# Running maximum of attention scores read from the SBUF copy instead of the PSUM bank

## The reference, cut to what matters

```python
kv = jnp.concatenate([context, latents], axis=1)        # 1857 rows of 512
q, k, v = latents @ Wq, kv @ Wk, kv @ Wv                # split into heads
q, k = rms_norm(q, q_norm_w), rms_norm(k, k_norm_w)
scores = jnp.einsum('bhgqd,bhkd->bhgqk', qg, k) / np.sqrt(128)
probs = jax.nn.softmax(scores, axis=-1)                 # max over the keys first
out = jnp.einsum('bhgqk,bhkd->bhgqd', probs, v)         # then out @ Wo
```

## Time and profile before

| what | value |
|---|---|
| median of three runs | 2953.23 us |
| the profiled execution's own time | 2952.19 us |
| its span, first to last instruction | 2950.4 us |
| busy: PE, DVE, ACT, POOL | 2800.4, 2178.1, 2069.0, 2418.5 us |
| mean granted TensorE clock | 0.965 of full speed |

### The profile page before, as it was taken

One profiled execution on the slowest core, in us unless ns is written; L12 is line 12 of the kernel. 1 busy time (PEld: TensorE's weight loads), 2 busy tenths in 40 slices (PEclk: granted clock), 3 DMA queues, 4 the chain that ended last, 5 costly groups with the idle time before them and its releaser, 6 DMA issues. The chain is left out here.

```text
span 2950.4 us, 46837 instructions
## 1 busy us (share of the span) xinstructions
PE 2800.4 (95%) x14860; PEld 2242.9 (76%) x14860; DVE 2178.1 (74%) x3447; ACT 2069.0 (70%) x3867; POOL 2418.5 (82%) x2271
## 2 busy tenths in 40 slices
PE   4669999999999999999999999999999999999976
PEld 2458888888888888888888888888888888888744
DVE  5677777777777777777777778777777777777855
ACT  2137777777777777777777777777777777777741
POOL 4548888888888888888988888888898888888880
PEclk7779999999999999999999999999999999999985
DMA  6224434333434433333434343334334333333101
GB/s 236 90 93 143 144 128 139 127 127 129 147 122 157 133 130 131 132 131 130 143 125 154 129 137 132 129 127 138 127 122 138 113 115 113 109 108 115 65 8 68
DMA packets 154885, 367.69 MB, mean 125 GB/s; under 512 B 12682, under 2 KB 46476, under 8 KB 154641
## 3 DMA queue, kind: packets, MB, share of 16 engines
q1 hardware_dynamic: 152888, 362.87, 37.1%
q10 hardware_dynamic: 1752, 1.84, 0.2%
HBM read 327.95 MB, written 36.70 MB: 124 GB/s over the span
## 5 line engine op out<-in xcount | busy, mean ns | idle before, releaser
L1170 DVE SCALAR_TENSOR_TENSOR running_max<-S_ps,rk,running_max 128x512 f32<-128x512 f32 (+1 forms) x896 | 669.6, 747 | 251.0 <-ACT scores L912 243.2
L912 ACT ACTIVATE scores<-S_ps,rk 128x512 f32<-128x512 f32 (+1 forms) x960 | 653.8, 681 | 225.9 <-PE S_ps L652 220.9
L570 POOL TENSOR_TENSOR P_lo<-late,P_hi 128x512 fp32r<-128x512 f32 x512 | 675.2, 1319 | 129.2 <-ACT late L928 129.2
L1154 DVE TENSOR_TENSOR scores<-scores,Mb_ps 128x512 f32<-128x512 f32 (+1 forms) x960 | 648.8, 677 | 166.4 <-PE Mb_ps L797 166.4
L588 POOL TENSOR_TENSOR late<-late,scores 128x512 f32<-128x512 f32 (+1 forms) x448 | 587.4, 1311 | 119.5 <-ACT scores L928 76.9
L650 PE MATMUL S_ps<-QT_hi,KT_hi 128*128 128x512 f32 (+1 forms) x960 | 560.3, 584 | 15.1 <-DVE running_max L1170 13.9
L588 POOL TENSOR_TENSOR late<-late 128x512 f32<-128x512 f32 x384 | 525.0, 1367 | 0.0
L650 PE MATMUL K_ps<-Wkv_hi,kvT 128*128 128x256 f32 (+1 forms) x1664 | 473.6, 285 | 2.9 <-DVE V_full L1210 2.9
L652 PE MATMUL K_ps<-Wkv_hi,kvT 128*128 128x256 f32 (+1 forms) x1664 | 473.7, 285 | 0.0
L651 PE MATMUL K_ps<-Wkv_lo,kvT 128*128 128x256 f32 (+1 forms) x1664 | 473.1, 284 | 0.0
L680 PE MATMUL OT_ps<-scores,V_full 128*128 128x512 f32 (+1 forms) x896 | 462.1, 598 | 0.0
(11 more groups left out here) (198 smaller groups left out, 5447.7 us busy)
## 6 DMA issues: line engine op xcount, KB each, us to landing
kvT<-kvT_scratch SPq DMA_DIRECT2D x416, 512.0 KB, 3.3
w_stage<-in_L_xattn_Wq SPq DMA_DIRECT2D x64, 512.0 KB, 4.3
w_stage<-in_L_xattn_Wo SPq DMA_DIRECT2D x64, 512.0 KB, 4.3
kvT_scratch<-built SPq DMA_DIRECT2D x58, 512.0 KB, 2.8
xrow<-in_ctx SPq DMA_DIRECT2D x48, 256.0 KB
w_stage<-in_L_xattn_Wk SPq DMA_DIRECT2D x32, 256.0 KB, 2.8
w_stage<-in_L_xattn_Wv SPq DMA_DIRECT2D x32, 256.0 KB, 3.3
xT<-kvT_scratch SPq DMA_DIRECT2D x6, 512.0 KB, 5.7
```

The costliest lines, as they stand in the source:

```text
L570: e.tensor_tensor(P_lo[n % 2][0:r, :], P_sb[n % 2][0:r, :], f(P_hi[n % 2][0:r, :]), ALU.subtract)\
L912: e.activation(row[s % RING][0:r, :], S_ps[s % 2][0:r, :], ACT.Copy, scale=rk[0:r, v % 2, j:j + 1])\
L1154: e.tensor_tensor(d, d, Mb_ps[0:r, :], ALU.add).then_inc(s_d, 1)
L1170: e.scalar_tensor_tensor(a, src, k, a, ALU.mult, ALU.max).then_inc(s_top, 1)
```

## The change

`raise_max` takes its source from the ring slot that ACT's copy has just filled instead of from the PSUM bank. The slot holds the scaled scores, so the multiplication by `rk` goes: the `scalar_tensor_tensor` of 14 tiles of a half becomes a `tensor_tensor` maximum of two SBUF operands, and the `tensor_scalar` of the first tile becomes a `tensor_copy` from SBUF to SBUF. DVE's running maximum no longer reads the bank, so PE's wait before it fills a bank again is on `s_cp` (ACT's copy of two steps before) instead of `s_top`. `rk` is no longer read by DVE, so POOL's wait on `s_top` before it writes `rk` goes too. Every engine has the same number of instructions in the same places as before.

```diff
@@ newton (POOL)
                 if kind != "q" and v >= 2:
 
                     e.wait_ge(s_cp, NJ * (2 * v - 2))
-                    e.wait_ge(s_top, NJ * (2 * v - 2))
                 e.tensor_tensor(r, a, y0, ALU.mult).then_inc(s_nw, 1)
@@ scores (PE)
                 if s >= 2:
 
-                    e.wait_ge(s_top, s - 1)
+                    e.wait_ge(s_cp, s - 1)
@@ raise_max (DVE)
                 a = top[0:r, :]
                 e.wait_ge(s_cp, s + 1)
-                src, k = S_ps[s % 2][0:r, :], rk[0:r, v % 2, j:j + 1]
+                src = row[s % RING][0:r, :]
                 if j == 0:
                     if p:
 
                         e.wait_ge(s_ff, F_AT["MT", p - 1] + 1)
-                    e.tensor_scalar(a, src, k, None, ALU.mult).then_inc(s_top, 1)
+                    e.tensor_copy(a, src).then_inc(s_top, 1)
                     return
                 e.wait_ge(s_top, s)
-                e.scalar_tensor_tensor(a, src, k, a, ALU.mult, ALU.max).then_inc(s_top, 1)
+                e.tensor_tensor(a, a, src, ALU.max).then_inc(s_top, 1)
```

## The result

The changed kernel takes 3142.24 us (median of four runs, 3140.86 to 3146.86) against 2952.64 us before (median of the three runs above and one beside it): 1.0645 times as long, 95% interval 1.063 to 1.0659. The forecast was 3175 us, slower, in a range of 3035 to 3345.

What follows compares the result with a forecast made beforehand. PE bounds the kernel at 83.7 us a unit; POOL would become the bound at 73.4 + 3.0 + 12.1 + 2.4 = 90.9, +7.2 over 31 units: 2952.2 + 223 = 3175 us, range 3035 to 3345.

Steps and rivals of the forecast that it cites:

- The maximum takes turns with POOL: DVE's maximum with two SBUF inputs and POOL's SBUF instructions run one after the other; maximum 1.2 to 1.6 us.
- POOL grows by 12.1 us a unit: POOL's cost of meetings: 28 maxima at 0.40 us and two SBUF copies at 0.45 us per unit.
- A third of POOL's waits stays, 2.4 us a unit: Of POOL's 7.3 us of waits for ACT per unit, 2.4 us remain, making the unit 90.9 us.
- The fixed gaps: Short gaps between POOL's own dependent instructions, 3.0 us a unit, which stay whatever happens.
- POOL, not DVE, sets the time: POOL becomes the bound at 90.9 us a unit, 60%; rival DVE at 94.8 us, 3296 us, 24%.
- The earlier bank: no effect: PE's bank returned after ACT's copy: at most 43.9 us, counted as nothing once PE isn't the bound.
- The wait that POOL loses: nothing: POOL's dropped wait before writing `rk` is for something two units old; no row shows a wait: nothing.

Runs made afterwards that it cites:

- POOL's length alone: Kernel before with two small POOL instructions (128x40) added in each step, DVE untouched: 3080.93 us, 1.0435.
- DVE's even length: Kernel before with one more DVE reduction of 256 columns after each maximum, POOL untouched: 2954.88 us, 1.0008.
- the two kernels with short additions: Changed kernel with POOL's additions from the third tile of a half on cut to 64 or 320 of 512 columns: 2940.0 and 2978.18 us.

## Why the prediction was right, step by step

- *The maximum takes turns with POOL.* Right, and for the reason given. Its mean of 1146 ns is a little under the forecast 1.2 to 1.6 us; its median is 1066. In the stretch from 200 to 3100 us 223 of 891 take under 0.72 us: they begin when POOL's instruction is over or nearly so, or meet POOL's tiny instructions. POOL's 1522 and 1607 ns, too, are at or under the low end of the forecast 1.6 to 1.75 us.
- *POOL grows by 12.1 us a unit.* It grew by 10.8, or 0.36 us for each of 30 instructions instead of 0.40 to 0.45, since not every one costs POOL, and the copy, taken at 0.45 us, costs it some 0.17 (last section).
- *A third of POOL's waits stays, 2.4 us a unit.* (48.7 + 14.3 + 6.3) / 32 = 2.2, the last term line 1044's 6.3 us. The fixed gaps stayed at 3.1 us. With 84.2 busy that is the unit of 89.5 us, and 5.8 x 31 = 180 of the 190 us. The sum had no term for the other 10, behind the last query scaling.
- *POOL, not DVE, sets the time.* Right. POOL's length alone gives 127 us, DVE's even length nothing. But the step goes by means per unit: with room for POOL in the mean it would have given no loss, and the two kernels with short additions still lose 20 and 24 us, in the one place where POOL is full.
- *The earlier bank: no effect.* This failed. It costs 15 to 20 us, by the two runs that undo it. The sum took it as nothing because PE isn't the bound; that PE's stops would get fewer and longer, and its granted clock lower after them, was not thought of.
- *The wait that POOL loses: nothing.* Undoing it as well gave 3121.5 instead of 3127.4 us, with overlapping intervals. ACT's new wait of 57 us for POOL's inverse norms comes from POOL's lateness, as the kernels with the old wait show it too (56.2 us in the first).

The forecast is 33 us too high: 1.4 us too many in each of 31 units make 43, and 10 outside the units were not counted. The units' 180 us also hold the 15 to 20 of the earlier bank. So POOL's terms were some 60 us too large, and two terms that stood at nothing made up for about half of that; that the number came so near is in part luck.

## What to carry to other kernels

Before moving an operand from PSUM to SBUF on DVE, count the SBUF inputs: with two of them the instruction takes turns with POOL's instructions on SBUF, and both engines get longer (here 0.75 to 1.15 us on DVE, 1.29 to 1.5 or 1.6 on POOL). Find a line of that kind in the trace and look at the POOL instruction beside it, both ends. Don't trust a mean busy share alone: look for the place of a unit where an engine has no wait between the input that it gets and the engine that waits for it. And releasing a buffer earlier to an engine that is not the bound can cost time: here its stops got fewer and longer, and its clock fell after the long one that was looked at.

## What was not expected of the hardware

A waiting maximum is not always next. At 1569.87 us one begins while POOL is in a pair of subtractions, and takes 3.48 us; POOL (second fence) finishes both and a whole addition, until 1572.81, before DVE ends at 1573.35, again 0.54 us later:

```profile
1569.87 3.48 DVE L1169 TENSOR_TENSOR running_max<-running_max,scores 128x512 f32<-128x512 f32 x1
```

```profile
1568.56 2.98 POOL L570 TENSOR_TENSOR P_lo<-late,P_hi 128x512 fp32r<-128x512 f32 x2
1571.51 1.30 POOL L584 TENSOR_TENSOR late<-late 128x512 f32<-128x512 f32 x1
```

Nine of 891 took over 3.3 us. "Who interferes with whom" in "SBUF — State Buffer" of the Trainium skill has the second engine blocked until the first one's instruction finishes; this one waited for three, so the measurement goes further. And the copy from SBUF to SBUF takes 0.42 us at best, where one of that size from PSUM takes 0.68, but it takes turns with POOL as the maximum does (median 1.10 us). One of them and POOL beside it:

```profile
530.18 1.15 DVE L1166 COPY running_max<-scores 128x512 f32<-128x512 f32 x1 [1.94 <-PE F_ps L787]
```

```profile
528.35 2.70 POOL L588 TENSOR_TENSOR late<-late,scores 128x512 f32<-128x512 f32 x2
531.01 2.57 POOL L626 TENSOR_TENSOR Wq_lo<-w_stage,Wq_hi 128x1024 fp32r<-128x1024 f32 x1
```

It ends at 531.33, 0.28 us after POOL's addition, and the weight split behind takes 2.57 us instead of the 2.40 of before.
